# Building an adjacency count matrix: eight edge chunks compared at once, in two interleaved halves, with GpSimd doing part of the subtraction

## The chip, the cores and the metric

The kernel runs on one NeuronCore of a Trainium2 chip. The metric is device time in microseconds (us); the figure compared is the median of several runs. A profile is one more execution, with its own time. Engines: TensorE (PE; its weight loads are PEld), VectorE (DVE), ScalarE (ACT), GpSimd (POOL), SyncE (SP), which only starts DMAs.

## The reference

A graph network: 3125 nodes with 128 features, and 103,125 directed edges (`src`, `dst`), sorted by `dst`. Four blocks follow each other, all on the same edges:

```
h = max(layernorm(x), 0);  x = x + sage2(h, edges)          # two mean aggregations
h = max(layernorm(x), 0);  x = x + hyperbolic(h, edges)
h = max(layernorm(x), 0);  x = x + sage3(h, edges)          # three more
h = max(layernorm(x), 0);  x = x + attention(h, edges)      # 8 heads, softmax over edges
```

Every aggregation but the attention's is `segment_sum(h[src], dst)`. That is a product with a matrix `counts[src, dst]`, which holds how many edges run from src to dst. The kernel builds this matrix once on the chip and then uses it in all dense aggregations.

## The kernel before

`program` runs three stages one after the other, with a barrier of all engines between them: `build_counts`, `dense_layers` and `attention`. Only `build_counts` differs between the two kernels.

`counts` lies in SBUF as 128 partitions (src modulo 128) by 25 blocks (src divided by 128) by 3136 columns (dst), in bf16. The edges are cut into chunks of 128, one edge in each partition. Because edges are sorted by dst, a pair of neighbouring chunks touches at most WP = 12 neighbouring dst columns, its window. For one pair (`q` in the code, 408 of them, two chunks each):

- **Right sides** (DVE, line 434). For each chunk a 128x300 one-hot (25 blocks by 12 window columns): `iota_b` compared with the edge's `key`, one tensor_scalar for each chunk, bf16 to bf16.
- **Left sides** (ACT, lines 462 and 470). For each chunk a 128x128 one-hot of `low` = src modulo 128, as `Relu(1 - (place - low)^2)`: a Square with a per-partition bias for each chunk, then one Relu over both chunks. Of every third pair the second chunk's left side is a comparison on DVE instead (line 432).
- **Product** (PE, line 496). Two matmuls accumulate left^T right into one of four PSUM banks `share`: 128x300.
- **Add** (DVE, line 449). The window of `counts` becomes the PSUM bank plus the window: one input in PSUM, one in SBUF, 128x300.

DVE issues, for a pair q, the right sides of pair q+2, then waits for `mm_done` and for `column_sums` (the add before it is complete), then adds pair q. It works in a hardware loop of TB = 34 turns of UB = 12 pairs; at the start of each turn it reads 24 window starts into registers (line 440), since an add's address is a register value. `left`, `right` and `square` have three slots each. POOL writes constants and clears half of `counts` ahead of the loop and does nothing in it. Ahead of the loop, too, DVE computes `key` and `low` (lines 378 to 402), then checks that the edges allow this method (lines 410 to 426); ACT starts as soon as the keys are there.

The helper `Num(c, k, m)` is an index: c, plus m for every loop turn k. `x.count(engine, sem)` makes the engine wait until `sem` has reached the value of x, and waits for nothing where c is not positive. `x.slot(n)` is c modulo n.

Of the kernel before, what the change touches and what calls it, by code (L numbers as in the profile page):

```python
# [35 lines left out]
UB = 12  # L36
# [240 lines left out]
def build_counts(nc, t, v, counts):  # L277
# [5 lines left out]
    RH, LH = 3, 3  # L283
    KW = NT * WP
    MID = KW // 2
    with ExitStack() as ctx:
# [9 lines left out]
        key = sb("key", [P, NC])  # L296
        pair_rel = dst_rows[:, :, :].rearrange("p g e -> p (g e)").bitcast(F32)
        low = sb("low", [P, NC])
        iota_b = sb("iota_b", [P, KW], BF16)
        one = sb("one", [P, 1])  # L300
        right = sb("right", [P, RH, 2, KW], BF16)
        square = sb("square", [P, 3, 2, P], BF16)
        left = sb("left", [P, LH, 2, P], BF16)
        share = ps("share", 4)
        flag_bank, = ps("flag_bank", 1)
        flat = sb("flat", [P, 3, NC], I32)
        test = sb("test", [P, 2, NC], BF16)
# [12 lines left out]
        def by_vector(q):  # L320

            return q.slot(3) == 2

# [5 lines left out]
        squares_ready, left_ready = sem("squares_ready"), sem("left_ready")  # L329
# [26 lines left out]
        def _(pool):  # L356
            chain = Chain(pool, pool_steps)
            chain.step(nc.gpsimd.iota(iota_i[:, :], [[1, KW]], base=-MID, channel_multiplier=0))
            chain.step(nc.gpsimd.tensor_copy(iota_b[:, :], iota_i[:, :]))
            chain.step(nc.gpsimd.memset(one[:, :], 1.0))  # L360
# [4 lines left out]
            nc.gpsimd.memset(counts[:, 0:half].bitcast(F32), 0.0).then_inc(column_sums, 1)  # L365
# [3 lines left out]
            chain.step(nc.gpsimd.tensor_copy(v.lane[:, :], v.lane[:, :].bitcast(I32)))  # L369

        @block.vector
        def _(dve):
# [29 lines left out]
            nc.vector.tensor_scalar(key[:, :], key[:, :], float(-MID), None, ALU.add).then_inc(keys_ready, 1)  # L402
# [25 lines left out]
            def right_sides(q):  # L428


                if by_vector(q):
                    nc.vector.tensor_scalar(left[:, q.slot(LH), 1, :], place, low[:, bass.ds(q.value(2) + 1, 1)], None, ALU.is_equal)
                for n in range(2):
                    nc.vector.tensor_scalar(right[:, q.slot(RH), n, :], iota_b[:, :], key[:, bass.ds(q.value(2) + n, 1)], None,  # L434
                                            ALU.is_equal).then_inc(right_ready, 1)

            right_sides(Num(0))
            right_sides(Num(1))
            with dve.Fori(0, TB) as k:
                _, first = nc.values_load_multi_w_load_instructions(  # L440
                    starts[0:1, bass.ds(k * (2 * UB), 2 * UB)], engines=(ENG.DVE,), min_val=0, max_val=NA - WP,
                    skip_runtime_bounds_check_because="bounded above by the min, below by the node numbers")
                for j in range(UB):
                    q = Num(j, k, UB)
                    right_sides(q + 2)
                    (q + 1).count(dve, mm_done)
                    (q + 1).count(dve, column_sums)
                    window = cols[:, :, bass.ds(first[2 * j], WP)]
                    nc.vector.tensor_tensor(window, share[j % 4][:, 0:KW].rearrange("p (t w) -> p t w", w=WP), window,  # L449
                                            ALU.add).then_inc(column_sums, 1)  # L450

        @block.scalar
        def _(act):
# [3 lines left out]
            def squares(q):  # L457

                (q - 2).count(act, left_ready)
                sides = 1 if by_vector(q) else 2  # L460
                for n in range(sides):
                    nc.scalar.activation(square[:, q.slot(3), n, :], place, ACT.Square, bias=low[:, bass.ds(q.value(2) + n, 1)],  # L462
                                         scale=-1.0).then_inc(squares_ready, 2 // sides)

            def one_hot(q):

                act.wait_ge(squares_ready, q.value(2) + 2)
                (q - (LH - 1)).count(act, mm_done)
# [1494 lines left out]
```

## Time and profile before

| | us |
|---|---|
| median of 3 runs (lowest 2685.66, highest 2693.41) | 2687.6 |
| the profiled execution's own time | 2701.79 |
| its span, first to last instruction | 2699.3 |
| in it: first right side starts | 43.72 |
| in it: last add of the build starts (0.46 long) | 448.97 |

The span is what the trace covers; the profiled execution's time is 2.49 us more. That execution is 14.2 us above the median of the runs. The build's loop is some 15% of the span; all that follows line 449 is the same in both kernels. A busy share is a mean over a stretch; where an engine's instructions overlap, the sum of their durations is more than its busy time.

### The profile page before, as it was taken

To read this page: it belongs to the slowest core of one execution; us is meant where nothing else is said; L and a number is where in the kernel's file an instruction comes from. 1 tells how busy PE (TensorE), PEld (TensorE's weight loads), DVE (VectorE), ACT (ScalarE), POOL (GpSimd) and SP (SyncE) were. 2 spreads that over 40 slices of the span, in tenths; PEclk is the share of its full clock that TensorE was granted. 3 is DMA by queue.
4 is the path that set the end of the run, shared out by engine and by line. 5 is a ranking of instruction groups with operands and counts; after the bars stand their busy time and mean duration, and the time that the engine had idled before them with its cause. 6 is when DMAs were issued, how large, how long until landed. Compare 5 with 4: busy or idle time off the path is not lost.

```text
span 2699.3 us, 48165 instructions
## 1 busy us (share of the span) xinstructions
PE 1760.8 (65%) x10229; PEld 1109.4 (41%) x10229; DVE 1418.9 (53%) x4461; ACT 1042.0 (39%) x3014; POOL 1025.5 (38%) x1355
## 2 busy tenths in 40 slices
PE   2666665699899999989355555645554555555554
PEld 0111111355555565656244444534344444444443
DVE  8888887433656533346244444534344444444444
ACT  3888886432554322212123223323223222233233
POOL 2000001322544310111455555565555655655552
PEclk9999999999999999999566666666666666666766
DMA  1000000100111101013433333333333333333331
GB/s 65 0 0 0 0 0 20 43 26 29 50 51 53 50 27 32 29 60 102 141 96 109 110 96 107 110 104 106 95 103 112 109 94 102 107 100 108 109 94 45
DMA packets 148866, 188.65 MB, mean 70 GB/s; under 512 B 25795, under 2 KB 117316, under 8 KB 148804
## 3 DMA queue, kind: packets, MB, share of 16 engines
q0 software_dynamic: 38784, 105.96, 13.5%
q1 hardware_dynamic: 110020, 82.00, 9.5%
q8 instruction: 23, 0.38, 0.1%
q14 instruction: 39, 0.32, 0.0%
HBM read 162.82 MB, written 25.04 MB: 70 GB/s over the span
## 4 chain that ended last, share of the span: by engine, by line
another core or an unknown queue 20%; DVE 13%; issue 10%; PE 7%; ACT 1%; DVEq 0%; DMA 0%; ACTq 0%
DVE counts L1460 4%; DVE a_score L1463 3%; PE aq_bank L1335 3%; PE acc_bank L1354 3%; DVE counts L1468 1%; DVE a_clipped L1473 1%; DVE counts L1392 1%; PE ap_bank L1341 0%; PE ac_bank L1370 0%; PE ac_bank L1371 0%; DVE counts L1416 0%; DVE a_stat L1424 0%; ACT counts L1300 0%; DVE a_stat L1423 0%
## 5 line engine op out<-in xcount | busy, mean ns | idle before, releaser
L1265 POOL DMA_INDIRECT counts<-keys_values,a_index x808 | 783.3, 969 | 576.9 <-ACT a_index L1280 340.6
L776 PE MATMUL z_bank<-y_parts,counts 128*128 128x384 bf16 (+1 forms) x3750 | 665.7, 329 | 4.1 <-DMA y_parts<-in_L_gnn_bq 4.1
L1335 PE MATMUL aq_bank<-counts 128*128 128x128 bf16 x2424 | 291.9, 263 | 356.6 <-issue 340.5
L1460 DVE TENSOR_TENSOR counts<-aq_bank,counts 128x512 f32<-128x512 f32 x202 | 139.3, 690 | 720.8 <-remote 602.5
L1354 PE MATMUL acc_bank<-counts 128*128 128x136 f32 x1616 | 338.9, 366 | 215.7 <-DVE counts L1468 107.9
L776 PEld LDWEIGHTS z_bank<-y_parts,counts 128*128 (+1 forms) x3750 | 370.0, 99 | 238.6 <-issue 14.1
L1296 ACT ACTIVATE counts<-a_clipped 128x32 f32<-128x32 f32 x202 | 46.1, 228 | 919.2 <-DVE a_clipped L1473 774.8
L1354 PEld LDWEIGHTS acc_bank<-counts 128*128 128x128 f32 x1616 | 288.5, 257 | 255.6 <-DVE counts L1468 129.6
L1335 PEld LDWEIGHTS aq_bank<-counts 128*128 128x128 bf16 x2424 | 211.6, 119 | 416.6 <-issue 406.3
L496 PE MATMUL share_build<-right_build,left_build 128*128 128x300 bf16 x816 | 276.9, 443 | 128.5 <-DVE right_build L434 98.0
L462 ACT ACTIVATE square_build<-iota_b_build,low_build 128x128 bf16<-128x128 bf16 x682 | 237.9, 387 | 2.2
L470 ACT ACTIVATE left_build<-square_build,one_build 128x256 bf16<-128x256 bf16 (+1 forms) x408 | 187.4, 459 | 55.5 <-PE share_build L496 55.4
L434 DVE TENSOR_SCALAR right_build<-iota_b_build,key_build 128x300 bf16<-128x300 bf16 x820 | 203.9, 291 | 0.1
L496 PEld LDWEIGHTS share_build<-right_build,left_build 128*128 128x128 bf16 x816 | 53.6, 110 | 351.8 <-ACT left_build L470 241.5
L449 DVE TENSOR_TENSOR counts<-share_build,counts 128x300 f32 x408 | 190.3, 466 | 0.0
L970 DVE TENSOR_REDUCE z_sum<-z_bank 128x128 f32<-128x384 f32 x150 | 83.6, 557 | 188.2 <-PE z_bank L776 187.1
L683 POOL MEMSET y_parts<- 128x50 bf16 x1 | 0.1, 143 | 430.8 <-POOLq L271 430.8
L1341 PE MATMUL ap_bank<-a_eye,counts 128*128 128x128 bf16 x808 | 113.7, 268 | 54.2 <-issue 53.7
L1463 DVE TENSOR_REDUCE a_score<-counts 128x32 f32<-128x512 f32 x202 | 138.6, 686 | 6.9
L764 PE MATMUL d_bank<-weights,hT 128*128 128x256 f32 x350 | 124.9, 442 | 22.8 <-ACT hT L852 21.8
L1468 DVE TENSOR_TENSOR counts<-counts 128x512 f32<-128x512 f32 x202 | 138.0, 683 | 0.0
L1300 ACT ACTIVATE counts<-ap_bank 128x512 f32<-128x512 f32 x202 | 117.2, 580 | 21.2 <-remote 18.6
(153 smaller groups left out, 1871.1 us busy)
## 6 DMA issues: line engine op xcount, KB each, us to landing
counts<-group_rel_rows SPq DMA_DIRECT2D x34, 768.0 KB
counts<-keys_values,a_index POOLq DMA_INDIRECT x808
self_term<-s_out SPq DMA_DIRECT2D x150, 64.0 KB, 1.6
s_in<-self_term SPq DMA_DIRECT2D x150, 64.0 KB, 1.8
residual<-x_in SPq DMA_DIRECT2D x75, 64.0 KB, 1.6
counts<-query_parts SPq DMA_DIRECT2D x34, 96.0 KB
x_in<-in_x SPq DMA_DIRECT2D x50, 64.0 KB, 1.8
x_in<-residual SPq DMA_DIRECT2D x50, 64.0 KB, 1.8
```

The lines of the kernel that those rows point to most:

```text
L434: nc.vector.tensor_scalar(right[:, q.slot(RH), n, :], iota_b[:, :], key[:, bass.ds(q.value(2) + n, 1)], None, ALU.is_equal).then_inc(right ...
L449: nc.vector.tensor_tensor(window, share[j % 4][:, 0:KW].rearrange("p (t w) -> p t w", w=WP), window, ALU.add).then_inc(column_sums, 1)
L462: nc.scalar.activation(square[:, q.slot(3), n, :], place, ACT.Square, bias=low[:, bass.ds(q.value(2) + n, 1)], scale=-1.0).then_inc(square ...
L470: nc.scalar.activation(left[:, q.slot(LH), 0:sides, :], square[:, q.slot(3), 0:sides, :], ACT.Relu, bias=one[:, :], scale=-1.0).then_inc(l ...
L496: ins = nc.tensor.matmul(share[j % 4][:, 0:KW], left[:, j % LH, n, :], right[:, j % RH, n, :], start=n == 0, stop=n == 1)
L776: yield s, nc.tensor.matmul(bank(p, dt)[:, 0:width], counts[:, bass.ds(dt.value(P) + s * NA, P)], y3[(p - 1) % 2][:, s, 0:width], start=s ...
L1265: nc.gpsimd.indirect_dma_start(rows_kv[:, j, c, :], None, v.kv, bass.IndirectOffsetOnAxis(index[:, j, c:c + 1], 0)).then_inc(gathered[j], 16)
L1335: ins = nc.tensor.matmul(q_bank[s.slot()][:, c * P:c * P + P], spread[:, g.slot(), (j * GC + c) * P:(j * GC + c) * P + P], queries[:, g.sl ...
L1354: ins = nc.tensor.matmul(acc_bank[ga.slot()][:, 0:TW], pick[:, s2.slot(3), c, :], msg[:, s2.slot(3), c, :], start=j == 2 and c == 0, stop= ...
L1460: nc.vector.tensor_tensor(prod[:, :].rearrange("p (c d) -> p c d", c=GC), q_bank[s.slot()][:, :].rearrange("p (c d) -> p c d", c=GC), rows ...
L1463: nc.vector.tensor_reduce(score[:, s.slot(), :], prod[:, :].rearrange("p (n d) -> p n d", d=DH), AX.X, ALU.add).then_inc(sum_done, 1)
L1468: nc.vector.tensor_tensor(wide[:, :, 0:D].rearrange("p c (h d) -> p c h d", h=H), rows_kv[:, (j - 1) % RG, :, D:2 * D].rearrange("p c (h d ...
```

## The change

The 816 chunks are taken as two streams of STREAM = 408 (the first and the second half of the edges). A **group** `g` is eight chunks, four neighbours of each stream, which is four pairs; there are 102 groups. UB becomes 8 pairs a turn (two groups), TB 51.

- DVE makes all eight right sides of a group with one tensor_tensor: `iota_wide` (each value four times in a row) against four neighbouring keys, now in bf16. The chunk is the innermost index, so that a matmul reads `right` with a step of four elements. There is no comparison for left sides on DVE any more.
- POOL subtracts for six of the eight chunks, `place - low`, in one tensor_tensor over 128x768 bf16. It waits for the right sides of the group before (`right_ready`) and until the Relu two groups back has read the slot (`left_ready`).
- ACT squares the two remaining chunks with a bias each, waits for POOL, squares the six in place, and issues one Relu over 128x1024.
- PE issues eight matmuls in a row into four of eight PSUM banks.
- DVE issues the right sides of group g+1 ahead of the four adds of group g. The adds alternate between the two streams, and `column_sums` starts at 2 instead of 1, so that an add waits for the add before the last one. Each turn reads 8 window starts, behind the turn's first comparison.
- Ahead of the loop: one more copy on POOL (`iota_wide`, 128x1200) and one more on DVE (`low_b`). Several tiles now share memory with tiles that are no longer in use.

```
-UB = 12
+UB = 8
+GB = 4
...
+            chain.step(nc.gpsimd.tensor_copy(iota_wide[:, :, :], iota_b[:, :].unsqueeze(2).to_broadcast([P, KW, 4])))
...
-            nc.gpsimd.memset(counts[:, 0:half].bitcast(F32), 0.0).then_inc(column_sums, 1)
+            nc.gpsimd.memset(counts[:, 0:half].bitcast(F32), 0.0).then_inc(column_sums, 2)
...
+            pool.wait_ge(keys_ready, 1)
+            def differences(g):
+                g.count(pool, right_ready)
+                (g - 1).count(pool, left_ready)
+                lows = low_b[:, 0:2 * STREAM].rearrange("p (h m) -> p h m", h=2)[:, :, bass.ds(g.value(GB), BY_POOL)]
+                nc.gpsimd.tensor_tensor(square[:, g.slot(), :, :].rearrange("p (h c) n -> p h c n", h=2)[:, :, 0:BY_POOL, :],
+                                        place.unsqueeze(1).unsqueeze(1).to_broadcast([P, 2, BY_POOL, P]),
+                                        lows.unsqueeze(3).to_broadcast([P, 2, BY_POOL, P]), ALU.subtract).then_inc(diff_ready, 1)
...
-            nc.vector.tensor_scalar(key[:, :], key[:, :], float(-MID), None, ALU.add).then_inc(keys_ready, 1)
+            chain.step(nc.vector.tensor_copy(low_b, low[:, :]))
+            nc.vector.tensor_scalar(key_b, key[:, :], float(-MID), None, ALU.add).then_inc(keys_ready, 1)
...
+            def sides(g):
+                keys = key_b[:, 0:2 * STREAM].rearrange("p (h m) -> p h m", h=2)[:, :, bass.ds(g.value(GB), GB)]
+                nc.vector.tensor_tensor(right[:, g.slot(), :, :, :], iota_wide[:, :, :].unsqueeze(1).to_broadcast([P, 2, KW, 4]),
+                                        keys.unsqueeze(2).to_broadcast([P, 2, KW, 4]), ALU.is_equal).then_inc(right_ready, 1)
+            def turn(k, last=False):
+                for j in range(UB // GB):
+                    if not (last and j == UB // GB - 1):
+                        sides(Num(j + 1, k, UB // GB))
+                    if j == 0:
...                                          # the 8 window starts
+                    for i in range(GB):
+                        q = Num(GB * j + i, k, UB)
+                        (q + 1).count(dve, mm_done)
+                        (q + 1).count(dve, column_sums)
+                        window = cols[:, :, bass.ds(first[i % 2 * (UB // 2) + 2 * j + i // 2], WP)]
+                        nc.vector.tensor_tensor(window, share[GB * j + i][:, 0:KW].rearrange("p (t w) -> p t w", w=WP), window,
+                                                ALU.add).then_inc(column_sums, 1)
...
+            def squares(g):
+                (g - 1).count(act, left_ready)
+                both = square[:, g.slot(), :, :].rearrange("p (h c) n -> p h (c n)", h=2)
+                for h in range(2):
+                    chunk = bass.ds(g.value(GB) + h * STREAM + BY_POOL, 1)
+                    nc.scalar.activation(both[:, h, BY_POOL * P:GB * P], place, ACT.Square, bias=low[:, chunk],
+                                         scale=-1.0).then_inc(squares_ready, 1)
+                (g + 1).count(act, diff_ready)
+                nc.scalar.activation(both[:, :, 0:BY_POOL * P], both[:, :, 0:BY_POOL * P], ACT.Square).then_inc(squares_ready, 1)
+            def one_hot(g):
+                act.wait_ge(squares_ready, g.value(3) + 3)
+                if g.c > 1:
+                    act.wait_ge(mm_done, (g - 1).value(GB))
+                nc.scalar.activation(left[g.slot()][:, :, :], square[:, g.slot(), :, :], ACT.Relu, bias=one[:, :],
+                                     scale=-1.0).then_inc(left_ready, 1)
+            def step(g):
+                squares(g + 1)
+                one_hot(g)
...
+                    pe.wait_ge(right_ready, g.value() + 1)
+                    (g + 1).count(pe, left_ready)
+                    for i in range(GB):
+                        for c in (i // 2 * 2, i // 2 * 2 + 1):
+                            ins = nc.tensor.matmul(share[j * GB + i][:, 0:KW], left[j][:, i % 2 * GB + c, :], right[:, j, i % 2, :, c],
+                                                   start=c % 2 == 0, stop=c % 2 == 1)
+                        ins.then_inc(mm_done, 1)
```

## Rows read from the trace of the kernel before

**Rows 1.** Windows by stage: us, busy of each engine (instructions), granted clock, DMA share, GB/s.
```profile
43.70:45.97 2.27, 1.18 (x4) 0.35 (x4) 0.92 (x4) 0.83 (x3) 0.00 (x0) 1.00 0.00 0
57.90:441.90 384.00, 262.44 (x774) 50.71 (x774) 331.31 (x1292) 335.28 (x1029) 0.00 (x0) 1.00 0.00 0
```
**Rows 2.** Waits of DVE, 40 to 450 us: total us, times, longest.
```profile
DVE left_build L432 <- issue: 55.5, 34, 1.7
```
**Rows 3.** Line 440 alone, on DVE's sequencer: ns min/median/max, first and last start.
```profile
L440 DVEq TENSOR_LOAD <-starts_build x34: 1599/1602/1871, 43.9 to 437.4; - x34
```
**Rows 4.** Timeline: start us, us, engine, line, what [idle before].
```profile
43.72 0.92 DVE L434 TENSOR_SCALAR right_build<-iota_b_build,key_build 128x300 bf16<-128x300 bf16 x4
...
45.97 0.26 DVE L432 TENSOR_SCALAR left_build<-iota_b_build,low_build 128x128 bf16<-128x128 bf16 x1 [1.33 <-issue]
...
200.13 0.49 ACT L470 ACTIVATE left_build<-square_build,one_build 128x256 bf16<-128x256 bf16 x1
200.53 0.68 ACT L462 ACTIVATE square_build<-iota_b_build,low_build 128x128 bf16<-128x128 bf16 x2
...
201.20 0.50 DVE L434 TENSOR_SCALAR right_build<-iota_b_build,key_build 128x300 bf16<-128x300 bf16 x2
201.62 0.47 DVE L449 TENSOR_TENSOR counts<-share_build,counts 128x300 f32 x1
201.83 0.68 PE L496 MATMUL share_build<-right_build,left_build 128*128 128x300 bf16 x2 [2.01 <-DVE right_build L434]
202.00 0.50 DVE L434 TENSOR_SCALAR right_build<-iota_b_build,key_build 128x300 bf16<-128x300 bf16 x2
...
439.17 0.25 DVE L432 TENSOR_SCALAR left_build<-iota_b_build,low_build 128x128 bf16<-128x128 bf16 x1 [1.64 <-issue]
...
448.97 0.46 DVE L449 TENSOR_TENSOR counts<-share_build,counts 128x300 f32 x1
```
**Rows 5.** Timeline, DVE ahead of the loop.
```profile
31.08 0.63 DVE L402 TENSOR_SCALAR key_build<-key_build 128x896 f32<-128x896 f32 x1
31.74 1.09 DVE L410 TENSOR_TENSOR test_build<-flat_build 128x896 bf16<-128x896 int32 x1
...
35.12 0.63 DVE L413 TENSOR_TENSOR test_build<-test_build 128x896 bf16<-128x896 bf16 x1
```
**Rows 6.** Groups by form: xcount | busy us, mean ns | idle before.
```profile
L725 POOL TENSOR_TENSOR s_out<-ys,bias_even 128x128 f32<-128x128 f32 x75 | 34.2, 456 | 133.5 <-ACT y_parts L861 116.4 <-issue 10.5 <-DVE stat L1007 4.1
L711 POOL TENSOR_SCALAR stat<-stat 128x1 f32<-128x1 f32 x100 | 23.4, 234 | 161.4 <-DVE stat L1007 141.1 <-issue 18.2
L369 POOL CAST lane_f<-lane_f 128x1 f32<-128x1 int32 x1 | 0.2, 188 | 0.1
L359 POOL CAST iota_b_build<-test_build 128x300 bf16<-128x300 int32 x1 | 0.4, 432 | 0.1
```
**Rows 7.** The same, ACT.
```profile
L462 ACT ACTIVATE square_build<-iota_b_build,low_build 128x128 bf16<-128x128 bf16 x682 | 237.9, 387 | 2.2
L470 ACT ACTIVATE left_build<-square_build,one_build 128x256 bf16<-128x256 bf16 x272 | 134.5, 494 | 8.3 <-PE share_build L496 8.2
L913 ACT ACTIVATE junk<-plain_h 128x128 bf16<-128x128 f32 x25 | 7.7, 309 | 0.8
```
**Rows 8.** Timeline of the dense stage: matmuls in a row.
```profile
619.18 2.97 PE L776 MATMUL z_bank<-y_parts,counts 128*128 128x385 bf16 x17
```
**Rows 9.** Timeline of the dense stage, where POOL and DVE add at once.
```profile
470.77 0.31 ACT L861 ACTIVATE y_parts<-ys 128x128 f32 x1
...
471.24 0.45 POOL L725 TENSOR_TENSOR s_out<-ys,bias_even 128x128 f32<-128x128 f32 x1 [0.91 <-ACT y_parts L861]
471.30 0.54 DVE L1038 TENSOR_TENSOR rest<-ys,y_parts 128x128 f32<-128x128 f32 x1 [0.19 <-ACT y_parts L861]
...
475.84 0.46 POOL L725 TENSOR_TENSOR s_out<-ys,bias_even 128x128 f32<-128x128 f32 x1 [0.99 <-ACT y_parts L861]
...
476.12 0.32 DVE L1038 TENSOR_TENSOR rest<-ys,y_parts 128x128 f32<-128x128 f32 x1
```

More of the change, by code:

```diff
@@ L369, in _ @@
             chain.step(nc.gpsimd.tensor_copy(v.lane[:, :], v.lane[:, :].bitcast(I32)))
+            pool.wait_ge(keys_ready, 1)
[7 more added lines that the diff above has]
+            for j in range(UB // GB):
+                differences(Num(j))
+            with pool.Fori(0, TB - 1) as k:
+                for j in range(UB // GB):
+                    differences(Num(UB // GB + j, k, UB // GB))
         @block.vector
@@ L426, in _ @@
             chain.step(nc.vector.tensor_tensor(v.odd[:, :], worst[0:1, 0:1], gap_flag[:, 0:1], ALU.max))
[L428 to L450, printed above, removed]
+            def sides(g):
+                keys = key_b[:, 0:2 * STREAM].rearrange("p (h m) -> p h m", h=2)[:, :, bass.ds(g.value(GB), GB)]
+                nc.vector.tensor_tensor(right[:, g.slot(), :, :, :], iota_wide[:, :, :].unsqueeze(1).to_broadcast([P, 2, KW, 4]),
+                                        keys.unsqueeze(2).to_broadcast([P, 2, KW, 4]), ALU.is_equal).then_inc(right_ready, 1)
@@ new lines, in turn @@
+            def turn(k, last=False):
+                for j in range(UB // GB):
+                    if not (last and j == UB // GB - 1):
+                        sides(Num(j + 1, k, UB // GB))
+                    if j == 0:
+                        pair_starts = starts[0:1, 0:2 * STREAM].rearrange("a (h m two) -> a h m two", h=2, two=2)
+                        _, first = nc.values_load_multi_w_load_instructions(
+                            pair_starts[:, :, bass.ds(k * (UB // 2), UB // 2), 0], engines=(ENG.DVE,), min_val=0, max_val=NA - WP,
+                            skip_runtime_bounds_check_because="bounded above by the min, below by the node numbers")
+                    for i in range(GB):
[5 more added lines that the diff above has]
+                                                ALU.add).then_inc(column_sums, 1)
@@ L452, in _ @@
+            sides(Num(0))
+            with dve.Fori(0, TB - 1) as k:
+                turn(k)
+            turn(TB - 1, True)
         @block.scalar
@@ L455, in _ @@
             act.wait_ge(keys_ready, 1)
[L457 to L468, printed above, removed]
-                sides = 1 if by_vector(q) else 2
-                nc.scalar.activation(left[:, q.slot(LH), 0:sides, :], square[:, q.slot(3), 0:sides, :], ACT.Relu, bias=one[:, :],
+            def squares(g):
[7 more added lines that the diff above has]
+                nc.scalar.activation(both[:, :, 0:BY_POOL * P], both[:, :, 0:BY_POOL * P], ACT.Square).then_inc(squares_ready, 1)
@@ L477, in _ @@
             squares(Num(0))
-            for j in range(UB):
+            for j in range(UB // GB):
                 step(Num(j))
-            with act.Fori(0, TB - 1) as k:
-                for j in range(UB):
-                    step(Num(UB + j, k, UB))
+            with act.Fori(0, TB - 2) as k:
+                for j in range(UB // GB):
+                    step(Num(UB // GB + j, k, UB // GB))
+            step(Num(UB // GB * TB - 2))
+            one_hot(Num(UB // GB * TB - 1))
         @block.tensor
```

40 lines of the change are left out of this document (18 added, 22 removed).

## The prediction

> **What bounds the kernel now.** I read the windows by stage first, for where the build lies and what is busy in it, then DVE's waits, then the timeline of single pairs, last the groups by form for durations.
>
> In the loop DVE is busy 331 and ACT 335 of 384.00 us, PE's granted clock is 1.00 throughout (the 2.4 GHz level), and POOL does nothing [rows 1]. ACT's share is high, but DVE sets the pace: in 40 to 450 us it waits for no engine, only for "issue", 55.5 us in 34 times [rows 2]. That is the reading of 24 window starts at each turn, 1.60 us on DVE's own sequencer [rows 3]. Between these stops, DVE goes from one pair's right sides to the next in 202.00 - 201.20 = 0.80 us [rows 4]; the extra comparison of every third pair adds 0.16 us (my reading of the turn: 12 x 0.79 + 4 x 0.16 + 1.64 = 11.8). A turn of 12 pairs is (439.17 - 45.97) / 33 = 11.92 us [rows 4], so **four pairs cost 3.97 us**. That is what a group of the new kernel has to beat. Loop and first comparison run from 43.72 to 449.43 us.
>
> **The change, part by part.** All times go against the profiled execution, 2701.79 us; the median of the runs is 14.2 us lower, and I carry the difference over to it.
>
> DVE, comparison. Removed for four pairs: eight tensor_scalars and 1.33 comparisons of left sides. Added: one tensor_tensor over 2400 bf16. The nearest row is the bf16 one over 896: 0.63 us [rows 5], against 1.09 for the same size on 32-bit inputs. The difference, 448 steps of 1.04 ns, says that bf16 goes two elements at a step, with 0.16 us fixed: 1.25 + 0.16 = **1.41 us**. The other end is one element at a step, 2.50 + 0.16 = 2.66 us: the row's inputs are dense, here one input repeats and the other comes in runs of four. I take 1.41, since every run is of adjacent 16-bit values.
>
> DVE, adds. The shape stays, 0.47 us, and the next instruction starts 0.38 us after an add starts [rows 4]. The add now waits only for the add before the last one, and so can still overlap with its neighbour: 4 x 0.385 = 1.54 us. With the wait for the neighbour it would be 4 x 0.50 (a waiting instruction starts 0.03 us after the end of the one before, [rows 5]: 31.08 + 0.63 to 31.74). DVE alone would need 1.54 + 1.33 = 2.87 us a group. The reading of 8 starts stands behind the comparison, which covers up to 1.4 us of it; beyond that it falls into DVE's wait for the matmuls, below. I cost it at nothing; without that cover it would be at most 51 x 1.6 us, less what the comparison hides, some 51 x 0.3 = 15 us.
>
> POOL. New: 102 subtractions over 768 bf16, two inputs. POOL does two-input work over 128 columns in 456 ns [rows 6], but only in f32. What part of that is fixed? One column costs 188 ns (a cast) or 234 ns (a tensor_scalar) [rows 6]; the slope is then 2.09 or 1.73 ns an element, and 768 elements cost 1.80 or 1.57 us. I take **1.70 us**. The ends: the one-input slope, (432 - 188) / 299 = 0.82 ns [rows 6], gives 0.81 us; six times the whole 456 ns gives 2.74 us.
>
> The Trainium skill (GPSIMD Engine Reference, section 3.1) gives a two-input add over 2048 f32 as 4497 ns and puts it down to one read interface that both inputs share. By an estimate from that and the 456 ns row the subtraction would take 1.80 us, and the sum below would come to some 2682 us instead of 2672.
>
> ACT. From the rows for 128 and 256 columns, 387 and 494 ns [rows 7], a column costs 0.836 ns. The Relu over 1024: 494 + 768 x 0.836 = 1.14 us. The Square over 768 has no pointer bias; the row without one is 309 ns for 128 [rows 7]: 309 + 535 = 0.84 us, of which the Relu behind it overlaps 0.10 (200.13 to 200.53 for one of 0.49, [rows 4]), leaves 0.74. The two with a bias, 0.29 + 0.39, are issued while POOL subtracts. ACT's own work is 0.03 + 0.58 + 0.74 + 1.14 = 2.5 us a group, less than now.
>
> PE. Eight matmuls in a row. The first pair ends some 0.65 us after it starts, and starts 0.12 us after what releases it (201.70 to 201.83, [rows 4]). In a row, 17 matmuls of 385 columns start 0.165 us apart [rows 8], so a pair of 300 columns follows each 0.28 us, less than an add's 0.385. If they stayed 0.24 us apart, as the two of a pair do now (0.68 - 0.44), or the step of four elements slowed the reading, adds would come each 0.48 us. I take no loss, for the ends see below.
>
> **What is late next.** No engine is full, so the chains decide. There are two.
>
> *Chain A, POOL and ACT.* The subtraction for group g+1 waits for the Relu of g-1, and the Relu of g stands on ACT behind the Square of g+1, which waits for that subtraction. From Relu to Relu: ACT to POOL 0.16 (471.08 to 471.24, [rows 9]), subtraction 1.70, to ACT 0.04 (estimate), Square 0.74, Relu 1.14: **3.78 us a group**.
>
> *Chain B, around DVE.* End of comparison g, 0.05, subtraction g+1 1.70, 0.04, Square 0.74, Relu g 1.14, PE 0.12 + 0.65 = 4.44 us until the first add of g may start; then four adds 1.54 and the comparison g+2 1.41. That is 7.39 us for two groups, 3.70 a group. (Adds each 0.48 us: 3.84.)
>
> So DVE's 2.87 is not reached, and chain A sets 3.78, against 3.97 before.
>
> The sum. DVE's new copy of `low` is 0.66 us ahead of the loop; POOL's copy of 1200 elements is 188 + 1200 x 0.82 = 1.2 us in the first 4 us and is waited for by nobody until 31.7. Comparison 0 ends at 43.72 + 0.66 + 1.41 = 45.79, the first add starts 4.44 later at 50.23, 101 groups on at 50.23 + 101 x 3.78 = 432.0, and the last add ends 1.62 later (3 x 0.385 + 0.47) at 433.6. Before, it was 449.43. The gain is **15.8 us**: 2686.0 for such an execution, **2671.8 for the median**. Behind the build nothing changes.
>
> POOL and DVE meet at the SBUF. Two adds of the dense stage show it: DVE's L1038 takes 0.54 us where it starts 0.06 after POOL's L725, and 0.32 where it starts 0.28 after [rows 9]; both times it ends 0.14 to 0.15 us after POOL's instruction. So DVE is held until POOL is through. In the new kernel a comparison and a subtraction would hold each other; by chain A the subtraction runs from 0.16 to 1.86 of a period, the adds from 0.77 to 2.3, the comparison from 2.3 to 3.7, and the next subtraction from 3.9. They do not meet, and I cost it at nothing. The Trainium skill (SBUF — State Buffer, section Who interferes with whom) says that a DVE instruction with two SBUF inputs and a GpSimd instruction that reads SBUF shut each other out for the whole instruction, while one with a single SBUF input does not; by that rule the first half agrees with the trace, and no run here shows the second.
>
> **The rivals.**
> - *POOL is quick on bf16.* For it: half the bytes an element. Against: no bf16 subtraction of POOL is in the trace. At 1.0 us, chain A is 3.08 and chain B (7.39 - 0.70) / 2 = 3.35 and decides: 49.53 + 101 x 3.35 + 1.62 = 389.5, gain 60, **2628**. At the lower end, 0.81, it is 2617.
> - *POOL is slow (the other side).* Chain A costs 101 us for each us of subtraction, and the gain is gone where it takes 1.86 us; over 1.94 it is a measurable loss. For it: the pattern has four dimensions and two repeated inputs, and only f32 rows of 128 are known. At 2.2 us: 50.73 + 101 x 4.28 + 1.62 = 484.6, **2723**; at the upper end, 2.74, it is 2778.
> - *The comparison goes one element at a step*, 2.66 us. Chain B becomes (7.39 + 1.25) / 2 = 4.32: 51.48 + 101 x 4.32 + 1.62 = 489.4, **2728**.
> - *The adds are shut out as well.* They read one operand from SBUF. If POOL and any DVE add excluded each other, a group would cost 1.70 + 0.14 + 2.87 + 0.05 = 4.76 us: 2771. Against it: so far only two inputs in SBUF show it.
>
> **How the numbers follow.** My forecast, a subtraction of 1.5 to 1.85 us, has 0.44, and its own range is 2650 to 2690. POOL quicker than that 0.22; POOL slower than 1.9 us 0.16; comparison at one element 0.07; adds shut out 0.06; the rest, 0.05, is PE or the sequencers taking the gain. A measurement of this kernel can tell 0.3% (8 us) from no change. The forecast's upper fifth and the 0.05 are within that; this gives faster 0.60, same 0.13, slower 0.27. The range that leaves out two in ten reaches from a subtraction of about 1.0 us to the comparison at one element: 2625 to 2730.
>
> **What would show it.** Right: a group of instructions of about 1.41 us for the comparison, 1.7 for POOL's subtraction, 0.84 and 1.14 on ACT; the adds 0.385 apart; DVE idle some 0.9 us a group, released by PE; POOL released by ACT, not by DVE; a period of 3.78 us. Wrong: a period that is not the sum of chain A's four terms; a subtraction that overlaps a comparison; or DVE without idle time, which would mean that the POOL term is far too big. A different duration of the subtraction moves the time by 1.0 us for each 10 ns, down to where chain B takes over (1.54 us), and by half of that below.

## The result: 0.6% slower, and the profile after

| | us |
|---|---|
| changed kernel, median of 8 runs (2705.28 to 2717.59) | 2709.41 |
| kernel before, 8 runs on the same chips (2685.66 to 2701.52) | 2694.67 |
| ratio, with its 95% interval (the two medians alone give 1.0055) | 1.0062 (1.0041 to 1.0082) |
| last add of the build ends, before / after | 449.43 / 462.26 |

The forecast was 2672 against 2687.6, a gain of 0.6%; the wide range, 2625 to 2730, held the time, the forecast's own, 2650 to 2690, did not, and its sign was wrong. In the profiled executions the build ends 12.8 us later, and all behind it takes 2249.9 us before and 2246.8 after. So the loss is in the build.

Windows of the changed kernel (columns as in [rows 1]): up to the first comparison, to the first add, the loop, the end. DVE falls from 86% busy [rows 1] to 77%, ACT from 87% to 64%; nobody is full. (The 1.00 of the clock column has no record behind it here, see "What spaces the matmuls".)

```profile
0.00:45.52 45.52, 0.59 (x2) 0.12 (x2) 38.68 (x38) 3.40 (x6) 22.32 (x16) 1.00 0.26 96
45.52:52.47 6.95, 0.84 (x4) 0.45 (x5) 2.73 (x3) 2.58 (x4) 3.35 (x2) 1.00 0.00 0
52.47:458.22 405.75, 229.10 (x802) 87.98 (x801) 313.92 (x501) 257.92 (x399) 146.32 (x100) 1.00 0.00 0
458.22:462.26 4.04, 3.44 (x13) 1.37 (x11) 3.67 (x8) 0.00 (x0) 0.00 (x0) 1.00 0.00 0
```

The third window is 100 groups, 4.06 us each, against 3.97 before and 3.78 forecast. Its waits, 60 to 430 us (total us, times, longest), answer to [rows 2]: DVE now waits for PE, and POOL for DVE's comparison, never for ACT's Relu.

```profile
POOL key_low_build L381 <- DVE flat_build L452: 237.9, 92, 2.9
ACT key_low_build L491 <- POOL key_low_build L381: 122.1, 91, 1.7
PE share_build L527 <- ACT left_build L498: 95.3, 46, 2.1
DVE counts L469 <- PE share_build L527: 75.9, 92, 0.9
```

One round of two groups in the timeline (start, length; L452 comparison, L381 subtraction, L491 and L498 Square and Relu, L527 matmuls, L469 adds):

```profile
201.58 2.29 PE L527 MATMUL share_build<-flat_build,left_build 128*128 128x300 bf16 x8 [2.10 <-ACT left_build L498]
...
201.79 1.47 POOL L381 TENSOR_TENSOR key_low_build<-iota_b_build,src_cols_build 128x768 bf16<-128x768 bf16 x1 [2.26 <-DVE flat_build L452]
202.41 2.07 DVE L469 TENSOR_TENSOR counts<-share_build,counts 128x300 f32 x4 [0.80 <-PE share_build L527]
...
204.51 1.41 DVE L452 TENSOR_TENSOR flat_build<-iota_wide_build,src_cols_build 128x2400 bf16<-128x2400 bf16 x1
...
205.32 2.29 PE L527 MATMUL share_build<-flat_build,src_tile_build 128*128 128x300 bf16 x8 [1.44 <-ACT src_tile_build L498]
206.18 1.47 POOL L381 TENSOR_TENSOR key_low_build<-iota_b_build,src_cols_build 128x768 bf16<-128x768 bf16 x1 [2.92 <-DVE flat_build L452]
206.78 1.64 DVE L469 TENSOR_TENSOR counts<-share_build,counts 128x300 f32 x4 [0.86 <-PE share_build L527]
207.68 0.84 ACT L491 ACTIVATE key_low_build<-key_low_build 128x768 bf16<-128x768 bf16 x1 [1.68 <-POOL key_low_build L381]
208.34 1.40 DVE L452 TENSOR_TENSOR flat_build<-iota_wide_build,src_cols_build 128x2400 bf16<-128x2400 bf16 x1
208.43 1.13 ACT L498 ACTIVATE left_build<-key_low_build,one_build 128x1024 bf16<-128x1024 bf16 x1
209.68 1.73 PEld L527 LDWEIGHTS share_build<-flat_build,left_build 128*128 128x128 bf16 x8 [2.65 <-issue]
209.71 2.29 PE L527 MATMUL share_build<-flat_build,left_build 128*128 128x300 bf16 x8 [2.10 <-ACT left_build L498]
```

Follow the comparison that ends at 205.92: subtraction to 207.65, Square and Relu to 209.56, matmuls from 209.71; adds start 0.83 later, take 2.07 (as at 202.41), the comparison behind them 1.41. That is the prediction's chain B, and it closes at 8.13 us for two groups. Eight matmuls take 2.29 us; with 0.44 for the last they start 0.264 us apart, a pair each 0.53, and the adds with them. (In the other group of a turn the adds start later but run closer; that chain has the same length.) At 206.78 the adds run 0.39 apart (1.64 for four), while the subtraction is under way: POOL does not hold adds.

What held those adds until 206.78 is not PE (its first pair was due at 206.15, 0.83 behind its start), but the read of the window starts, on DVE's sequencer from 204.6; it answers to [rows 3]:

```profile
L461 DVEq TENSOR_LOAD <-starts_build x49: 1852/1855/1870, 58.4 to 448.4; - x49
```

Eight values take longer than 24 did. Ahead of the loop, POOL's first subtraction (34.8 its end) holds a check of the edges for 1.15 us, by the mechanism of [rows 9] (its like without a subtraction beside it takes 1.09):

```profile
32.51 2.30 POOL L381 TENSOR_TENSOR key_low_build<-iota_b_build,src_cols_build 128x768 bf16<-128x768 bf16 x1 [11.18 <-DVE src_cols_build L423]
33.52 2.24 DVE L432 TENSOR_TENSOR test_build<-flat_build 128x896 bf16<-128x896 int32 x1
```

### The profile page after: what moved, and what is told of

The parts are those of the page before. It is cut to its first block, busy times and chain, and to the rows that moved or that the text cites. A ratio compares the mean times of both kernels' runs of the same rounds, so it can differ in the third digit from the quotient of the medians.

```text
span 2709.1 us, 44819 instructions
## 1 busy us (share of the span) xinstructions
PE 1718.8 (63%) x10229; PEld 1147.5 (42%) x10229; DVE 1390.7 (51%) x3608; ACT 948.5 (35%) x2332; POOL 1183.3 (44%) x1458
## 4 chain that ended last, share of the span: by engine, by line
another core or an unknown queue 17%; DVE 12%; issue 11%; PE 10%; ACT 1%; DMA 0%; DVEq 0%; POOL 0%; ACTq 0%
PE acc_bank L1385 4%; PE aq_bank L1366 4%; DVE counts L1491 3%; DVE a_score L1494 3%; DVE counts L1499 1%; PE ap_bank L1372 1%; DVE a_clipped L1504 1%; DVE counts L1423 1%; PE ac_bank L1402 0%; PE ac_bank L1401 0%; DVE a_stat L1455 0%; DVE counts L1447 0%; DVE a_stat L1454 0%; ACT L1320 0%
## 5 line engine op out<-in xcount | busy, mean ns | idle before, releaser
L1385 PE MATMUL acc_bank<-counts 128*128 128x136 f32 x1616 | 346.8, 369 | 239.3 <-issue 129.7
L1366 PE MATMUL aq_bank<-counts 128*128 128x128 bf16 x2424 | 285.0, 263 | 314.2 <-issue 299.3
L381 POOL TENSOR_TENSOR key_low_build<-iota_b_build,src_cols_build 128x768 bf16<-128x768 bf16 x102 | 152.0, 1490 | 281.9 <-DVE flat_build L452 268.6
L469 DVE TENSOR_TENSOR counts<-share_build,counts 128x300 f32 x408 | 181.9, 473 | 95.0 <-PE share_build L527 85.6
L527 PE MATMUL share_build<-flat_build,left_build 128*128 128x300 bf16 x408 | 116.8, 443 | 102.9 <-ACT left_build L498 102.9
L527 PE MATMUL share_build<-flat_build,src_tile_build 128*128 128x300 bf16 x408 | 116.8, 443 | 80.7 <-ACT src_tile_build L498 78.6
L452 DVE TENSOR_TENSOR flat_build<-iota_wide_build,src_cols_build 128x2400 bf16<-128x2400 bf16 x102 | 142.9, 1402 | 1.5
L491 ACT ACTIVATE key_low_build<-key_low_build 128x768 bf16<-128x768 bf16 x102 | 86.0, 843 | 147.8 <-POOL key_low_build L381 147.8
L527 PEld LDWEIGHTS share_build<-flat_build,left_build 128*128 128x128 bf16 x408 | 44.7, 118 | 174.6 <-issue 130.6
```

Source lines behind the costliest of these rows:

```text
L381: nc.gpsimd.tensor_tensor(square[:, g.slot(), :, :].rearrange("p (h c) n -> p h c n", h=2)[:, :, 0:BY_POOL, :], place.unsqueeze(1).unsquee ...
L452: nc.vector.tensor_tensor(right[:, g.slot(), :, :, :], iota_wide[:, :, :].unsqueeze(1).to_broadcast([P, 2, KW, 4]), keys.unsqueeze(2).to_b ...
L469: nc.vector.tensor_tensor(window, share[GB * j + i][:, 0:KW].rearrange("p (t w) -> p t w", w=WP), window, ALU.add).then_inc(column_sums, 1)
L527: ins = nc.tensor.matmul(share[j * GB + i][:, 0:KW], left[j][:, i % 2 * GB + c, :], right[:, j, i % 2, :, c], start=c % 2 == 0, stop=c % 2 ...
L1366: ins = nc.tensor.matmul(q_bank[s.slot()][:, c * P:c * P + P], spread[:, g.slot(), (j * GC + c) * P:(j * GC + c) * P + P], queries[:, g.sl ...
L1385: ins = nc.tensor.matmul(acc_bank[ga.slot()][:, 0:TW], pick[:, s2.slot(3), c, :], msg[:, s2.slot(3), c, :], start=j == 2 and c == 0, stop= ...
```

## The experiments

They ran on two kinds of chip: the kernel before takes some 2690 us on one (the changed kernel, e1, e2, e3, e5 and e15) and 2384 on the other (all others). Each ratio is to the kernel before on the same kind of chip, so ratios from the two kinds are not compared with each other; the period of a group, read from the trace, is. The changed kernel has 4.06 us and 1.0062. Edits are to the changed kernel unless another is named. Theory P: chain B sets the pace. It has three handles: POOL's wait for the comparison, the length of POOL's and ACT's work, and the spacing of the matmuls.

**The wait for the comparison (e3_no_right_wait).**
```
             def differences(g):
-                g.count(pool, right_ready)
                 (g - 1).count(pool, left_ready)
```


> GpSimd's subtraction no longer waits for the comparison of the group before; the wait for the Relu two groups back stays and guards the slot. Theory P (the chain comparison, subtraction, Square, Relu, matmul, adds, comparison sets the pace, 8.12 us for two groups): the chain is cut, what is left is Relu to Relu, 0.16 + 1.47 + 0.03 + 0.75 + 1.13 = 3.54 us a group, plus up to 0.3 where a subtraction and a comparison now hold each other: 3.6 to 3.85, 20 to 45 us less than the changed kernel, ratio to before 0.99 to 0.998. Theory D (the pace is set on VectorE and TensorE, subtraction off the path): period stays 4.06, ratio 1.006. Theory H (the mutual holding is what the wait avoids, and is dearer): comparisons of 1.4 + 1.5 us and a slower kernel, ratio over 1.01.

Measured: 0.9867 (0.9813 to 0.9922), 36 us less than the kernel before. Timeline:

```profile
201.22 1.47 POOL L380 TENSOR_TENSOR key_low_build<-iota_b_build,src_cols_build 128x768 bf16<-128x768 bf16 x1 [2.09 <-ACT left_build L497]
202.15 1.81 DVE L451 TENSOR_TENSOR flat_build<-iota_wide_build,src_cols_build 128x2400 bf16<-128x2400 bf16 x1
...
203.88 1.59 DVE L468 TENSOR_TENSOR counts<-share_build,counts 128x300 f32 x4
...
204.79 1.47 POOL L380 TENSOR_TENSOR key_low_build<-iota_b_build,src_cols_build 128x768 bf16<-128x768 bf16 x1 [2.10 <-ACT src_tile_build L497]
205.42 2.11 DVE L451 TENSOR_TENSOR flat_build<-iota_wide_build,src_cols_build 128x2400 bf16<-128x2400 bf16 x1
```
From subtraction to subtraction 3.57 us, and POOL is now released by ACT: that is chain A with its measured terms, 0.16 + 1.47 + 0.03 + 0.75 + 1.13 = 3.54. The comparisons are held (1.95 us in the mean instead of 1.40), and this costs next to nothing, since they are off the path. In the loop DVE writes nothing that the subtraction reads and does not touch what it writes, so this wait guards no data. It keeps the two engines apart, and turned a gain of 1.3% into a loss of 0.6%. Theory D falls, and so does H.

**POOL out of the loop (e5_no_gpsimd).**
```
-                for h in range(2): ... one Square with a bias; wait for diff_ready; one Square over the six
+                for h in range(2):
+                    for c in range(GB):
+                        ... one Square with a bias
```


> GpSimd does nothing in the loop; ScalarE squares all eight chunks with a bias each. Theory P: ScalarE sets the pace, 8 x 0.29 + 0.10 + 1.13 + 0.03 = 3.58 us a group, 0.48 less than with GpSimd's help, 49 us less in all: ratio to before about 0.988. Theory D (VectorE and TensorE set the pace): 4.06 and 1.006. Theory A (ScalarE was the bound and GpSimd relieves it): slower than the changed kernel, ratio over 1.01.

Measured: 0.9858 (0.9802 to 0.9915), 3.62 us a group (PE's eight start at 201.62 and 205.24). ACT, at 96% busy, is the bound, and still a group takes 0.44 us less than with POOL's help, 11% of a period: with the wait for the comparison in place, the help cost more in handing over than it saved. Without that wait (e3, 3.57 us) it comes out even.

**A smaller share for POOL (e4_four_by_pool).** BY_POOL 2, four Squares with a bias.

> GpSimd subtracts for four of eight chunks (512 columns) and ScalarE squares the other four with a bias each; both waits of the subtraction stay. Theory P: the subtraction is shorter by a third, some 1.04 us instead of 1.47, the Square behind it 0.63 instead of 0.84; the chain is 0.64 us shorter for two groups... that is (8.12 - 0.64) / 2 = 3.74 us a group, some 32 us less than the changed kernel, ratio to before 0.994. Theory A (GpSimd's share relieves ScalarE, so more work for ScalarE costs time): slower than the changed kernel.

Measured: 0.9931 (0.9914 to 0.9948), 3.74 us a group (91 subtractions in 340 us). The subtraction over 512 took 1.04 us, that over 768 1.47: 1.67 ns an element and 0.19 fixed. Theory A falls.

**The adds' wait (e11_adds_in_order).** `then_inc(column_sums, 2)` back to 1.

> column_sums starts at 1 again: each add waits for the add just before it. Prediction's price: 0.115 us for each add that is not held by TensorE. Theory P: in the odd groups the adds follow matmuls 0.53 us apart and nothing changes; in the even groups, whose adds start late behind the read of the window starts and then run 0.385 apart, three gaps grow to 0.50: 0.35 us on a chain of 8.12, that is 4.23 us a group, 18 us more than the changed kernel, ratio to before 1.013. Rival: no chain is touched, ratio 1.006.

Measured: 1.018 (1.0163 to 1.0197), 4.32 us. The direction is P's, the size was not: adds that wait for their neighbour start 0.67 us apart, with 0.20 of idle time each, not 0.50:

```profile
203.78 0.47 DVE L469 TENSOR_TENSOR counts<-share_build,counts 128x300 f32 x1
...
204.45 0.49 DVE L469 TENSOR_TENSOR counts<-share_build,counts 128x300 f32 x1 [0.20 <-DVE counts L469]
205.14 0.47 DVE L469 TENSOR_TENSOR counts<-share_build,counts 128x300 f32 x1 [0.20 <-DVE counts L469]
```
So the looser wait, which taking the two halves in turn allows, is worth 0.26 us a group, 27 us in all or about 1%.

**The read of the window starts (e7_load_hoisted).** Read once ahead of the loop; all turns then use the first windows.

> The window starts are read once ahead of the loop (so all turns add into the windows of the first; every instruction else stays). Theory P: of the two chains that alternate, only the one of the even groups meets the read (its adds start 1.46 us behind TensorE's start instead of 0.83, but then run 0.385 apart instead of 0.53), and both have 8.12 us; without the read neither is shorter by more than 0.1: 4.03 to 4.06 us a group, within 0.2% of the changed kernel, ratio 1.003 to 1.007. Theory V (the read of 1.85 us stops VectorE, as it did 34 times before): 51 x 0.6 = 32 us less, ratio 0.994.

Measured: 1.0084 (1.0067 to 1.0101), 4.06 us (84 subtractions in 340 us, as in the changed kernel). The period is P's: the read, though it holds DVE 0.6 us a turn, is on no chain here. Theory V falls. The ratio is 0.1% above what I gave, but it is of the 2384 us: 20 us, where the interval of the changed kernel spans 11 to 22. That shows no difference.

**What spaces the matmuls.** Seven runs. First the right sides read contiguously (e1_contiguous), or constants in PE's idle time (e2_filler; e6_filler16 with 16):
```
-  right[:, j, i % 2, :, c],
+  right[:, j, i % 2, :, :].rearrange("p n c -> p (n c)")[:, c * KW:c * KW + KW],      # e1
+  for _ in range(6):                                                                  # e2; 16 in e6
+      nc.tensor.matmul(share[j * GB][:, 0:KW], place, iota_b[:, :], start=True, stop=True)
```


> The matmuls read 300 neighbouring elements of the right sides instead of every fourth (so the products are of other elements; the comparison is unchanged). Theory S, the step of four slows TensorE: the eight matmuls of a group, 0.264 us apart after the change, come 0.14 to 0.17 apart, the adds 0.385 instead of 0.53, the period of a group falls from 4.06 to about 3.85 us, some 20 us less in all. Theory L, what spaces them is something else that any short burst of matmuls pays (the pair of the kernel before is 0.24 us apart too, and reads neighbouring elements): spacing 0.24 to 0.264, period 4.0 to 4.06, time within 0.3% of the changed kernel, that is 1.003 to 1.009 of the kernel before.

> Six more matmuls of 300 columns a group, from constants into a bank that the group overwrites, issued in TensorE's idle time between the comparison's end and the Relu's. They take 1.6 us at most of a gap of 1.9 us. Theory L (a TensorE that has just been idle runs its first matmuls apart): real matmuls closer than 0.264 us, towards the 0.165 of the dense stage, adds 0.385 apart, first add 0.65 instead of 0.83 us behind TensorE's start; per group (0.56 + 0.2) / 2 = 0.38 us less, some 39 us less in all than the changed kernel, ratio to the kernel before about 0.992. If the spacing is fixed by the weights' load or the step of four: no difference, ratio 1.006.

> As the run with six more matmuls a group, now sixteen, so that TensorE has next to no gap ahead of the group's own eight. In the run with six, the six came 0.126 us apart behind the eight, and the eight still 0.264 apart behind a gap of 0.7 to 1.2 us. Theory G (matmuls run at half rate behind a gap, at 300 columns in 0.25 us, whatever their step): the eight now come about 0.13 apart, the adds 0.385, and the period falls below 3.9 us where the fillers don't delay the eight. Theory R (the eight are slow for what they read or signal: other weights each, a step of four, a signal for each pair): still 0.264 apart, period 4.0 or, where sixteen more are in the way, longer.

Measured: e1 1.0043 (1.0016 to 1.007), spacing 0.244, 4.00 us. e2 1.0042 (1.0018 to 1.0067), 4.02 us, spacing of the group's own unchanged. Its trace also records the clock. Two windows (columns as in [rows 1]) and PE's timeline in them (L525 the six constants, L529 the group's own eight):

```profile
129.60:132.80 3.20, 3.20 (x13) 1.49 (x12) 2.27 (x4) 2.32 (x4) 0.69 (x1) 0.50 0.00 0
133.00:138.00 5.00, 3.79 (x20) 1.81 (x18) 4.16 (x9) 3.22 (x5) 2.06 (x2) 1.00 0.00 0
```
```profile
129.63 1.68 PE L525 MATMUL share_build<-iota_b_build 128*128 128x300 bf16 x6
131.28 2.30 PE L529 MATMUL share_build<-flat_build,src_tile_build 128*128 128x300 bf16 x8
133.40 0.95 PE L525 MATMUL share_build<-iota_b_build 128*128 128x300 bf16 x6
135.56 2.29 PE L529 MATMUL share_build<-flat_build,left_build 128*128 128x300 bf16 x8 [1.21 <-ACT left_build L498]
```
Where the granted clock is 1.00 (2.4 GHz), the six constants start 0.13 us apart ((0.95 - 0.29) / 5; a single one then takes 0.29); where it is 0.50 (1.2 GHz), 0.245 ((1.68 - 0.456) / 5; a single one takes 0.456). The group's own eight have 0.264 at either level. With sixteen constants, PE has no gap (340.00 of 340.00 us busy), and the eight still have 0.264; 1.0135 (1.0114 to 1.0155), 4.17 us. So neither edit alone does it, and I first took both suspects as cleared. They were not. With a constant left side (e9_const_left, one run) the spacing stays 0.264, with a constant contiguous right side (e10_const_right, one run) it is 0.244, as in e1 (4.06 and 4.00 us a group):

> The eight matmuls of a group take a constant tile for the left side instead of the Relu's output (so the counts are others); waits, signals, banks and the right sides stay. If what is read as the left side (another weight each, written by ScalarE just before) spaces the matmuls at 0.264 us, they now come 0.13 apart; if the right sides or the pair-wise accumulation and signals do, still 0.26.

> The same with a constant, contiguous 300-column tile for the right side and the real left sides. With a contiguous read of the real right sides the spacing was 0.244. If the right sides (their place in memory, written by VectorE just before) are what slows, 0.13; if the pair-wise accumulation into one bank or the signals are, 0.24 again.

Then four kinds of constants in one kernel (e13_kinds_of_fillers; L525 pairs in one bank, L527 four banks, L529 a step of four, L531 a signal each, L535 the group's own):

> Eighteen extra matmuls a group from constants, of four kinds, ahead of the group's own: six that accumulate in pairs in one bank; four that go to four banks; four whose right side is read with a step of four elements; four that each signal a semaphore. Plain ones came 0.127 us apart, the group's own 0.264, with constant operands too. The kind that comes 0.24 to 0.26 apart names what spaces the group's own. Theory Acc (pairs in one bank): the six at 0.24. Theory Bank: the second four. Theory Step: the third four at 0.26 (then the 0.244 with a contiguous read is still to be explained). Theory Sig: the last four. If none does, something of the group that none of the four has is the cause.

```profile
203.26 0.95 PE L525 MATMUL share_build<-iota_b_build 128*128 128x300 bf16 x6
204.04 0.67 PE L527 MATMUL share_build<-iota_b_build 128*128 128x300 bf16 x4
204.55 1.23 PE L529 MATMUL share_build<-iota_wide_build,iota_b_build 128*128 128x300 bf16 x4
205.60 0.69 PE L531 MATMUL share_build<-iota_b_build 128*128 128x300 bf16 x4
```
Only the step of four is slow: (1.23 - 0.44) / 3 = 0.26 us, the others 0.13. Left was why contiguous ones in e1 and e10 have 0.244. So both at once (e15_contiguous_no_gap):

> Both suspects away at once: the matmuls read 300 neighbouring elements of the right sides (other elements, so other products), and sixteen constant matmuls a group fill TensorE's gap. Theory Two (a step of four, and a gap ahead, each alone halve a matmul's rate): the group's own eight come 0.127 to 0.14 apart, where each edit alone left 0.244 and 0.264; the adds come 0.385 apart, TensorE's start to the first add falls from 0.83 to about 0.65 us, and a group takes 3.75 to 3.85 us, ratio to before about 0.995. Theory One (the step alone; the contiguous 0.244 comes from the group's own signals and banks): still 0.24, period 4.0.

```profile
204.86 1.20 PE L529 MATMUL share_build<-flat_build,src_tile_build 128*128 128x300 bf16 x8 [0.50 <-ACT src_tile_build L498]
204.99 1.47 POOL L381 TENSOR_TENSOR key_low_build<-iota_b_build,src_cols_build 128x768 bf16<-128x768 bf16 x1 [2.10 <-ACT src_tile_build L498]
```
Now (1.20 - 0.29) / 7 = 0.13 us; 0.9875 (0.9807 to 0.9944), and a group takes 3.64 us. **Two causes, either one enough:** the step of four, and TensorE's lower clock level. The run was planned to fill a gap, but it isn't the gap just ahead that counts: here PE still stood idle 0.50 us ahead of the eight, in the kernel before 0.28 or less ahead of most pairs, and their two matmuls start 0.22 to 0.24 apart all the same. What the sixteen constants changed is the clock. The trace of e15 records it at 1.00 from 52.8 to 424.8 us. The traces of e1, of the changed kernel and of the kernel before hold no record of it in the build at all (the first is at 520.9, 461.2 and 516.5 us), and where there is none, the column prints 1.00. The 0.244 of e1 is the spacing that e2 has at 0.50; so e1 ran its build at 1.2 GHz, which is worked out from the spacing, not recorded. The Trainium skill (TensorE: Matmul & The Clock Gate, Part 1: The HAM clock gate) describes a gate that sets TensorE's clock by how busy the engine has been, and calls the throttled level the default; the runs agree, 0.244 us without the constants and 0.13 with them.

**A faster version (e8_pool4_free, e12_four_groups_a_turn, e14_starts_packed).** e8 is e3 and e4 together:

> Both edits at once: GpSimd subtracts for four of eight chunks, and does not wait for the comparison. Theory P: Relu to Relu is now the longer of GpSimd's 0.16 + 1.04 + 0.03 and ScalarE's own four Squares, 1.26, then 0.53 + 1.13: some 2.95 us; VectorE then sets the pace, 1.54 + 1.33 plus the holds of a comparison by a subtraction (0.54 of each comparison in the run with six chunks, in proportion to 1.04 us of subtraction some 0.3): 3.2 to 3.3 us a group, some 30 us less than the run without the wait alone, ratio to before 0.975 to 0.98. Rival: TensorE's eight matmuls at 0.264 us (2.1 us) and the adds behind them keep it at 3.5: ratio 0.986.

Measured: 0.9759 (0.9743 to 0.9775), 3.35 us. Here the read is on the path: DVE stands idle 0.87 us behind a comparison in every other group. Reading less often made it worse:

> The run with four chunks by GpSimd and no wait for the comparison, with four groups a turn instead of two (UB 16, TB 26: 832 chunks, two groups more), so that the window starts are read 26 times instead of 51. In that run VectorE waits 0.87 us for the read once in two groups, and a group takes 3.35 us. Theory P: the read is on VectorE's path now; saved are 25 x 0.87 = 22 us, paid are two groups, 6 us: 15 us less, ratio to before about 0.970. Rival: the wait hides another (TensorE's eight matmuls), and the two groups more are all that is seen: 0.978.

Measured: 0.9941 (0.9924 to 0.9957), 3.73 us: sixteen values took 3.62 us, not the 1.86 that I had assumed. So the cost goes by value, 0.23 us with a step of two in two rows, 0.07 for neighbours (24 in 1.60, [rows 3]). e14 is e8 with the starts copied once into reading order:
```
+            for h in range(2):
+                chain.step(nc.vector.tensor_copy(turn_starts[...(k h m), half h], starts[...every second of half h]))
...
-                            pair_starts[:, :, bass.ds(k * (UB // 2), UB // 2), 0], ...
+                            turn_starts[0:1, bass.ds(k * UB, UB)], ...
```


> The run with four chunks by GpSimd and no wait for the comparison, and the window starts copied once into the order in which the turns read them, so that each turn reads 8 neighbouring values. The read of 24 neighbours took 1.60 us, of 8 with a step of two in two rows 1.86, of 16 such 3.62. Theory N (a read costs by value, 0.07 us for a neighbour, 0.22 with a step): the read takes 0.55 to 0.7 us, is hidden by the comparison, VectorE's 0.87 us of waiting once in two groups goes, and a group takes 2.97 us instead of 3.35 (ScalarE's own period in that run where nothing holds it: 2.97): some 38 us less, ratio to before 0.960. Theory F (a read has a fixed cost of some 1.5 us): read 1.6, period 3.3, ratio 0.975.

Measured: **0.961 (0.9594 to 0.9626)**, the same output: 94 us less than the kernel before. (The changed kernel was measured on the other kind of chip, at some 15 us more than the kernel before.) The read takes 0.60 us, and a group 2.97, against 4.06. DVE is now busy all of 60 to 330 us and ACT 257.20 of these 270:

```profile
L460 DVEq TENSOR_LOAD <-turn_starts_build x47: 594/597/601, 61.6 to 334.9; - x47
```
```profile
202.90 1.04 POOL L381 TENSOR_TENSOR key_low_build<-iota_b_build,src_cols_build 128x512 bf16<-128x512 bf16 x1 [1.95 <-ACT src_tile_build L502]
...
205.87 1.04 POOL L381 TENSOR_TENSOR key_low_build<-iota_b_build,src_cols_build 128x512 bf16<-128x512 bf16 x1 [1.92 <-ACT left_build L502]
```

## Why the prediction was wrong

The two chains, the account of DVE alone and the sum's form were right; the sign turned on the terms of chain B, above all on one, and so on which chain was longer.

- **Comparison**: forecast 1.41 us, measured 1.40. Two elements at a step also with a repeated and a run-of-four input. Right.
- **Subtraction**: forecast 1.70, measured 1.47 (1.67 ns an element where the f32 row gave 2.09 with the same fixed part). By itself this would have been a further gain. The estimate from the figure of the Trainium skill (GPSIMD Engine Reference, section 3.1), 1.80, was farther off.
- **Square, Relu**: 0.84 and 1.14, measured 0.84 and 1.13. Right.
- **Chain A**: forecast 3.78, with the measured subtraction 3.54; e3 shows it at 3.57. The chain was right, but it was not the longer one.
- **Chain B**, the step that failed. Forecast 7.39, measured 8.13 for two groups: adds + 0.56, first add behind PE's start + 0.18, DVE to POOL + 0.21 (0.26 instead of 0.05), PE's start + 0.03, subtraction - 0.23, the rest - 0.01; sum + 0.74. The prediction said of the matmuls "I take no loss", and took 0.165 us for 385 columns from [rows 8], some 0.13 for 300 (a pair each 0.26, where it wrote 0.28, which changes nothing). The pair of this very loop already had 0.24 [rows 4]; measured was 0.264. The hand-over to POOL, 0.05, came from no row; its row for ACT to POOL has 0.16. It had named both the step of four and 0.24 as ways to 0.48 us an add, and priced them (3.84 us), but only with the other terms as they were. Behind it lies a misreading: it took the 1.00 of [rows 1] for the 2.4 GHz level, but that trace records no clock before 516.5 us, and the 0.24 of the pair is the 1.2 GHz spacing. [rows 8] lies in a stretch that is recorded at 1.00, and reads neighbours; here neither is so. e13 shows what the step does, e2 and e15 what the clock does; e15, with both away, brings a group from 4.06 to 3.64 us.
- **Adds**: that the wait for the add before the last lets them overlap is right (0.385 to 0.39 where PE is ahead); the price of the other wait was too low, 0.50 against 0.67 (e11).
- **The read of window starts**, costed at nothing: right for this kernel (e7), for a wrong reason. I had it no dearer than before, 1.6 us at most; it took 1.86, and DVE's slack paid. In e8 the slack was gone and it cost 0.4 us a group.
- **Start**: first add forecast at 50.23, was at 52.47. The subtraction and DVE's work ahead of the loop held each other, 1.15 us once, and POOL's second one was held 1.1 us by the comparison of group 1. I had looked for such meetings in the loop only.
- **Rivals**: POOL was quick (1.47, between my forecast and the rival's 1.0) and the kernel slower all the same; none of the slower rivals was what happened. "Adds shut out" falls: adds run 0.39 apart within a subtraction. The Trainium skill (SBUF — State Buffer, section Who interferes with whom) has it so for a DVE instruction with a single SBUF input, which no row of before could show. The matmuls' spacing should have been a rival of its own, with chain B in front: 3.84 us at least, and 4.06 with the terms as measured.
- **Range and chances**: that 2625 to 2730 held 2709 is luck. Its upper part was there for a slow subtraction or comparison, and neither was slow. By its own parts the chances come to faster 0.57, same 0.14, slower 0.29, not 0.60, 0.13, 0.27.

## What to carry to other kernels

Work handed to an idle engine is priced by the loop that it closes, not by the engines' sums: here the hand-over of a group's work through POOL and back, closed by a wait for DVE, cost more than ACT doing it alone (4.06 against 3.62 us). Take a wait that only keeps two engines apart as a suspect: let them collide, and see whether the held one was on the path. For the rate of a burst of matmuls use a row with the same step and the same clock level. Check that the level is recorded in that stretch: the spacing of contiguous matmuls tells it, 0.13 against 0.245 us for 300 columns.

## What the runs showed that I had not expected

- A matmul that reads its moving operand with a step of four bf16 (8 bytes) takes twice the time a column at the 2.4 GHz level: 0.26 us for 300 against 0.13 (e13). At the 1.2 GHz level the two hardly differ: 0.264 against 0.245 (e2).
- Eight contiguous matmuls of a group come 0.244 us apart where PE is idle 1.58 to 2.10 us ahead of them, and 0.13 where constants leave it 0.33 to 0.50 us and the clock is recorded at 1.00 (e1, e15).
- A granted clock of 1.00 can stand for no record. The build of e3, e5, e8, e12 and e14 is recorded at 0.50; in the changed kernel the column reads 1.00, with none before 461.2 us, and the strided matmuls have the same 0.264 us apart in all of them. Nothing shows that its clock was another than theirs. Window 60 to 400 of e3:

```profile
60.00:400.00 340.00, 218.22 (x763) 84.23 (x761) 331.24 (x478) 245.64 (x382) 139.62 (x95) 0.50 0.00 0
```
  What raises the clock, other than constants in PE's idle time, was not tried, nor a kernel with e14's edits that also reads contiguously.
- Reading values into registers costs 0.23 us each with a step of two in two rows, 0.07 for neighbours (e12, e14). Which of the step and the two rows costs was not tried apart.
- GpSimd's two-input bf16 subtraction costs 0.19 us and 1.67 ns an element (512 and 768 columns).
